# Mixed expert blocks without register loads, answers fetched in 2 KB pieces, and a wider GpSimd add in the first combine

## The reference, cut to what matters

```python
def ffn(x):                      # x normalised, 4096 x 256
    scores = sigmoid(x @ gate.T)                         # 32 experts
    topk_idx = top_k(masked(scores + bias), 6)           # 6 experts per token
    for e in range(32):                                  # gate_up[e]: 256 x 256, down[e]: 256 x 128
        o = (silu(x @ gu[e][:128].T) * (x @ gu[e][128:].T)) @ down[e].T
        routed += combine[:, e] * o                      # zero where e was not chosen
    return routed + (silu(x @ sg.T) * (x @ su.T)) @ sd.T # shared expert
x = x + 0.5 * ffn(layernorm(x))
x = x + local_attention(layernorm(x), segments of 64) + global_attention(segment means)
x = x + 0.5 * ffn(layernorm(x))
```

## Time and profile before

| | |
|---|---|
| median of three runs | 1494.6 us (1494.43 to 1495.4) |
| profiled execution | 1491.28 us, its span 1489.4 us |
| granted TensorE clock | 0.911 of full speed |
| PE busy | 1265.4 us, 85% |
| DVE busy | 1057.8 us, 71% |
| POOL busy | 894.5 us, 60% |
| ACT busy | 720.5 us, 48% |
| DMA, mean | 184 GB/s |
| answers fetched, first combine | 32 DMAs of 512 KB, 32 of 256 KB, about 5 us each from issue to landing |

### The profile page before, as it was taken

How to read it: one execution, slowest core, us unless ns; L and a number is a source line. 1 busy time by engine, 2 the same in 40 slices (tenths; PEclk the granted TensorE clock), 3 DMA queues, 4 the chain that set the end, 5 groups by cost and what they waited for, 6 DMA issues and landing times. The chain is left out here.

```text
span 1489.4 us, 47447 instructions
## 1 busy us (share of the span) xinstructions
PE 1265.4 (85%) x10480; PEld 1077.5 (72%) x10481; DVE 1057.8 (71%) x5308; ACT 720.5 (48%) x2232; POOL 894.5 (60%) x949
## 2 busy tenths in 40 slices
PE   6876662699999999789989989942999999999984
PEld 5765661599999996478766767732999999984864
DVE  6676656488888886477478888864788888874775
ACT  3433320466666665300467666721666666664100
POOL 3777777466666665332027776774666666654786
PEclk8777775799999999999799999955999999999998
DMA  9963333466666665597013333453666666653896
GB/s 312 404 263 128 128 128 128 138 189 187 188 190 189 188 190 167 162 329 249 2 47 133 141 137 129 147 190 132 183 192 190 189 189 193 189 181 112 301 317 221
DMA packets 154761, 274.44 MB, mean 184 GB/s; under 512 B 27942, under 2 KB 107067, under 8 KB 154688
## 3 DMA queue, kind: packets, MB, share of 16 engines
q1 hardware_dynamic: 116288, 160.27, 35.2%
q0 software_dynamic: 38400, 113.31, 20.5%
HBM read 146.59 MB, written 131.07 MB: 186 GB/s over the span
## 5 line engine op out<-in xcount | busy, mean ns | idle before, releaser
L772 PE MATMUL ps<-xbt,ans 128*128 128x128 f32 x3072 | 409.2, 276 | 0.2
L772 PEld LDWEIGHTS ps<-xbt,ans 128*128 128x128 f32 x3072 | 376.3, 193 | 1.3 <-ACT ans L1375 0.8
L733 POOL DMA_INDIRECT answers<-yb,didx x208 | 204.9, 985 | 159.2 <-issue 102.4
L733 POOL DMA_INDIRECT answers<-ans,didx x208 | 204.8, 985 | 128.8 <-issue 87.6
L717 POOL DMA_INDIRECT dispatch_rows<-blk,idx x192 | 190.6, 993 | 137.1 <-issue 121.9
L1375 ACT COPY ans<-wgu 128x512 f32 x416 | 255.2, 614 | 0.2 <-issue 0.2
L1864 DVE SCALAR_TENSOR_TENSOR picked<-iota_e,etab,blk 128x32 f32<-128x32 f32 x832 | 177.0, 250 | 102.7 <-DVE yb L1885 36.4
L693 POOL DMA_INDIRECT dispatch_rows<-blk,idx x192 | 188.0, 979 | 78.3 <-issue 58.1
L772 PE MATMUL ps<-wdn,hb 128*128 x768 | 229.6, 381 | 0.0
L1385 ACT ACTIVATE sg<-ps 128x128 f32<-128x128 f32 x416 | 115.8, 278 | 210.0 <-PE ps L772 206.5
L1367 ACT COPY xbt<-ps 128x256 f32<-128x256 f32 x416 | 153.9, 370 | 76.7 <-PE ps L895 76.6
(11 more groups left out here) (272 smaller groups left out, 2188.5 us busy)
## 6 DMA issues: line engine op xcount, KB each, us to landing
blk<-dispatch_rows SPq DMA_DIRECT2D x384, 160.0 KB
ans<-answers SPq DMA_DIRECT2D x54, 512.0 KB, 5.0
ans<-answers SPq DMA_DIRECT2D x54, 256.0 KB, 5.0
wgu<-in_gate_up SPq DMA_DIRECT2D x32, 256.0 KB
dispatch_rows<-blk,idx POOLq DMA_INDIRECT x384
dispatch_rows<-padt SPq DMA_DIRECT2D x32, 160.0 KB
blk<-dispatch_rows SPq DMA_DIRECT2D x64, 80.0 KB
yb<-answers SPq DMA_DIRECT2D x10, 512.0 KB, 5.3
```

The lines of the kernel that those rows point to most:

```text
L733: pool.indirect_dma_start(out=answers_dram, out_offset=bass.IndirectOffsetOnAxis(ap=didx[:, q:q + 1], axis=0), in_=block_answers(q), in_of ...
L772: return nc.tensor.matmul(out_, lhs, rhs, start=start, stop=stop)
```

## The change

It has three parts.

**Mixed blocks.** SP, PE and ACT hold all the register values of the 16 mixed blocks in registers of their own, read from `itab` while whole blocks are still worked on. SP's last 60 whole blocks are written out, and each carries one piece of that: the load of a register or, every other block, one of the first twelve down-weight loads, which now have twelve buffers. The last four follow between mixed row loads. Two semaphores take the place of four: one for the first twelve, one for the last four.

**2 KB pieces.** All fetches of answers are DMAs of 2 KB a partition (256 KB in all), three a tile, in both combines.

**First combine.** There are four buffers. PE sums answers 0 and 1 by two matmuls with the identity. POOL adds answers 2 and 3 to answers 4 and 5 in one instruction of 512 elements. PE adds the first half of that to its sum with one more matmul (`pooled`, issued behind the next tile's `first_two`), and DVE adds the second half to `xres` as before. SP fetches the third piece of tile i when PE (`four`) and DVE (`own`) are done with tile i-4.

```diff
-        def upper_down(k):
-            return vv[:, k, :] if k < 2 else prob[:].rearrange("p h k -> p (h k)")[:, (k - 2) * D:(k - 1) * D]
+        def upper_down(m):
+            k = m % DOWNS
+            if k >= 10:
+                return (xn2, red[:])[k - 10]
+            return (vv[:].rearrange("p k d -> p (k d)"), prob[:].rearrange("p h k -> p (h k)"),
+                    hsh[:].rearrange("p j s -> p (j s)"), ssg[:].rearrange("p j s -> p (j s)"),
+                    flat[:, E * E + 4 * P + 2 * KC * 2 * I:])[k // 2][:, k % 2 * D:(k % 2 + 1) * D]
...
+        held = [flat[:, 0:6 * D], flat[:, 6 * D:], (yb[:].rearrange("p k d -> p (k d)"), vv[:]),
+                (blk[:].rearrange("p q r -> p (q r)"), prob[:])]
...
             def load_mixed(m):
                 n = WHOLE + m
                 freed(n)
                 for k in range(2):
-                    reg = ahead[(2 * m + k) % 16]
                     sp.dma_start(block_rows(n % LOADS)[k * SEG:(k + 1) * SEG, :],
-                                 rows_dram[bass.ds(row_of(reg), SEG), :]).then_inc(s.ld[n % LOADS], 16)
-                    if m + 8 < MIXED:
-                        fetch(reg, WHOLE + 2 * (m + 8) + k)
+                                 rows_dram[bass.ds(row_of(ahead[2 * m + k]), SEG), :]).then_inc(s.ld[n % LOADS], 16)
...
-            for k, n in enumerate(range(WHOLE - 4 * LOADS, WHOLE)):
-                load(n, n % LOADS, m=0)
-                fetch(ahead[k], WHOLE + k)
-            for m in range(4):
-                load_down(m)
-            for m in range(MIXED + 4):
-                if m < MIXED:
-                    load_mixed(m)
-                if m >= 8:
-                    load_down(m - 4)
+            for n in range(WHOLE - peeled, WHOLE):
+                load(n, n % LOADS, m=0)
+                k = n - (WHOLE - peeled)
+                if k < 2 * DOWNS:
+                    (load_down if k % 2 else fetch_upper)(k // 2)
+                elif k < DOWNS + MIXED:
+                    fetch_upper(k - DOWNS)
+                else:
+                    fetch(ahead[k - (DOWNS + MIXED)], WHOLE + k - (DOWNS + MIXED))
+            for m in range(MIXED):
+                load_mixed(m)
+                if 9 <= m < 9 + MIXED - DOWNS:
+                    load_down(DOWNS + m - 9)
...
             for i in range(NT):
-                j = i % 3
-                positive(sp, s.four, i - 2)
-                sp.dma_start(sums_of[j][0], ans_v[i][:, 0:4 * D]).then_inc(s.ans[0][j], 16)
-                positive(sp, s.own, i - 2)
-                sp.dma_start(sums_of[j][1], ans_v[i][:, 4 * D:]).then_inc(s.ans[1][j], 16)
+                j = i % 4
+                two = lambda k: ans_v[i][:, 2 * k * D:(2 * k + 2) * D]
+                positive(sp, s.two, i - 3)
+                sp.dma_start(two_of(j, 0), two(0)).then_inc(s.ans[0][j], 16)
+                positive(sp, s.pair, i - 3)
+                sp.dma_start(two_of(j, 1), two(1)).then_inc(s.ans[1][j], 16)
+                positive(sp, s.four, i - 3)
+                positive(sp, s.own, i - 3)
+                sp.dma_start(two_of(j, 2), two(2)).then_inc(s.ans[1][j], 16)
...
         def pool_sum(pool, s):
             for i in range(NT):
-                two = sums_of[i % 3][1]
-                pool.wait_ge(s.ans[1][i % 3], 16 * (i // 3 + 1))
-                pool.tensor_tensor(two[:, 0:D], two[:, 0:D], two[:, D:], ALU.add).then_inc(s.pair, 1)
+                pool.wait_ge(s.ans[1][i % 4], 32 * (i // 4 + 1))
+                pool.tensor_tensor(two_of(i % 4, 2), two_of(i % 4, 1), two_of(i % 4, 2), ALU.add).then_inc(s.pair, 1)
...
-                for k in range(4):
-                    m = mm(ps[:, q, 0:D], ident[:], four[:, k * D:(k + 1) * D], start=(k == 0), stop=(k == 3))
-                m.then_inc(s.four, 1)
+                for k in range(2):
+                    m = mm(ps[:, q, 0:D], ident[:], two_of(i % 4, 0)[:, k * D:(k + 1) * D], start=(k == 0), stop=False)
+                m.then_inc(s.two, 1)
+
+            def pooled(i, q):
+                pe.wait_ge(s.pair, i + 1)
+                mm(ps[:, q, 0:D], ident[:], two_of(i % 4, 2)[:, 0:D], start=False).then_inc(s.four, 1)
...
-            act.wait_ge(C0.own, NT - 2)
+            act.wait_ge(C0.own, NT - 1)
+            act.wait_ge(C0.four, NT - 1)
```

More of the change, by code:

```diff
@@ L361, in __init__ @@
                     self.sh_x = s("sh_x")
-        LOADS, ANSWERS = 4, 8
+        LOADS, ANSWERS, DOWNS = 4, 8, 12
         row_loads = [sem(f"ex_ld{q}") for q in range(LOADS)]
-        down_loads = [sem(f"ex_dn{q}") for q in range(4)]
+        first_downs, last_downs = sem("ex_first_downs"), sem("ex_last_downs")
         class ExpertSems:
@@ L412, in __init__ @@
                 s = lambda name: sem(f"{name}_0")
-                self.ans = [[s(f"cs_ans{part}_{j}") for j in range(3)] for part in range(2)]
+                self.ans = [[s(f"cs_ans{part}_{j}") for j in range(4)] for part in range(2)]
+                self.two = s("cs_two")
                 self.four = s("cs_four")
@@ L524, in sp_experts @@
             first = [sp.alloc_register(f"first{k}_{s.n}") for k in range(2)]
-            ahead = [sp.alloc_register(f"first_half{k}_{s.n}") for k in range(16)]
+            ahead = [sp.alloc_register(f"first_half{k}_{s.n}") for k in range(2 * MIXED)]
             def fetch(reg, n):
@@ L885, in pe_experts @@
             expert = [pe.alloc_register(f"expert{j}_{s.n}") for j in range(2)]
-            lower = [pe.alloc_register(f"lower_expert{j}_{s.n}") for j in range(3)]
+            lower = [pe.alloc_register(f"lower_expert{j}_{s.n}") for j in range(MIXED)]
             pe.wait_ge(s.tab, 1)
@@ L956, in step @@
                     pe.reg_load(expert[1 - j], itab[0:1, bass.ds(n - 1, 1)])
-                if m is not None and WHOLE <= n + 1 < NB:
-                    mixed_expert(n + 1)
+                if m is not None and WHOLE <= n + MIXED < NB:
+                    mixed_expert(n + MIXED)
             tx(0, 0)
@@ L967, in pe_experts_run @@
                 step(n, n, m=0)
-            with pe.Fori(1, WHOLE // 8 - 1) as g:
+            with pe.Fori(1, (WHOLE - MIXED) // 8) as g:
                 for q in range(8):
                     step(g * 8 + q, q)
-            for n in range(WHOLE - 8, NB + 2):
+            for n in range(WHOLE - MIXED, NB + 2):
                 step(n, n % 8, m=0)
@@ L1025, in pe_sum @@
             for i in range(NT):
-                body(i, i % 4)
+                first_two(i, i % 4)
+                if i:
+                    pooled(i - 1, (i - 1) % 4)
                 if i >= 10:
@@ L1035, in pe_sum @@
                     pe_qk(pe, 2, 1, 0, 0, FIRST_K)
+            pooled(NT - 1, (NT - 1) % 4)
             mean(NT - 10)
@@ L1369, in act_experts, with stage @@
             expert = [act.alloc_register(f"staged_expert{j}_{s.n}") for j in range(2)]
-            def stage(n, j):
-                e = act.snap(expert[j], min_val=0, max_val=E - 1)
+            upper = [act.alloc_register(f"staged_upper{j}_{s.n}") for j in range(MIXED)]
+            def stage(n, j, m):
+                mixed = m is not None and n >= WHOLE
+                e = act.snap(upper[n - WHOLE] if mixed else expert[j], min_val=0, max_val=E - 1)
                 positive(act, s.gu, n - 1)
@@ L1391, in step @@
                     xt_copy(n + 2, j)
-                if m is not None and WHOLE <= n + 3 < NB:
-                    act.reg_load(expert[1 - j], itab[0:1, bass.ds(2 * (n + 3) - WHOLE + 1, 1)])
-                elif m is None or n + 3 < NB:
+                if m is None or n + 3 < WHOLE:
                     act.reg_load(expert[1 - j], itab[0:1, bass.ds(n + 3, 1)])
+                if m is not None and WHOLE <= n + MIXED + 4 < NB:
+                    act.reg_load(upper[n + MIXED + 4 - WHOLE], itab[0:1, bass.ds(2 * (n + MIXED + 4) - WHOLE + 1, 1)])
             act.wait_ge(s.tab, 1)
@@ L1401, in act_experts @@
             xt_copy(0, 0)
-            stage(0, 0)
+            stage(0, 0, 0)
             xt_copy(1, 1)
-            stage(1, 1)
+            stage(1, 1, 0)
             act.reg_load(expert[0], itab[0:1, 2:3])
@@ L1407, in act_experts @@
                 step(n, n, m=0)
-            with act.Fori(1, WHOLE // 4 - 1) as g:
+            with act.Fori(1, (WHOLE - MIXED) // 4 - 1) as g:
                 for q in range(4):
                     step(g * 4 + q, q)
-            for n in range(WHOLE - 4, NB):
+            for n in range(WHOLE - MIXED - 4, NB):
                 step(n, n % 4, m=0)
@@ L1904, in own @@
                 v.wait_ge(s.pair, i + 1)
-                v.tensor_tensor(xtile(i), sums_of[i % 3][1][:, 0:D], xtile(i), ALU.add).then_inc(s.own, 1)
+                v.tensor_tensor(xtile(i), two_of(i % 4, 2)[:, D:], xtile(i), ALU.add).then_inc(s.own, 1)
             def stats_of(i):
```

55 lines of the change are left out of this document (30 added, 25 removed).

## The result

| | before | with the change |
|---|---|---|
| median of 20 runs | 1492.19 us (1480.58 to 1495.96) | 1497.7 us (1490.0 to 1504.03) |
| ratio | | 1.0038, 95% interval 1.0023 to 1.0052 |
| profiled execution | 1491.28 us | 1492.44 us |

The change makes the kernel 5.5 us slower. The forecast was -0.3 us, so it was wrong in sign, and the case that I called C, +5.8 us, is what the time looks like. It doesn't follow that C's mechanism is what happened, and it isn't quite. The time itself, 1497.7 us, lies inside the forecast's own range of 1489.5 to 1499, but by luck: the kernel before came out 2.4 us lower in 20 runs than in the three that the forecast started from. Note that the change's profiled execution lies 5.3 us under its own median, while that of before lies 0.9 under.

What follows compares the result with a forecast made beforehand. It took late loads to stall PE at mixed blocks, a three-buffer fetch loop to bound the first combine, and POOL the second. -8.2 + 7.5 + 0.4 = -0.3 us gave 1494.3 us, range 1489.5 to 1499.

Steps and rivals of the forecast that it cites:

- C: First combine: every POOL add holds DVE for all of its 1.08 us, 3.025 us a tile; 1500.4 us, chance 0.22.
- Mixed blocks, -8.2: End of both expert stages: moving down-weight and register loads away removes PE's waits and the irregular steps behind them, -8.2 us.
- rival D: Last 60 whole blocks of each layer: SP falls behind with the moved loads, +6 us; about 1500.3 us, chance 0.04.
- First combine, +7.5: First combine: POOL's longer add holds up DVE, which becomes the bound at 2.79 us a tile; +7.5 us in all.
- -2.05 forecast: Start of the first combine: four tiles fetched at once bring tile 5's `own` to 636.3 instead of 638.35, -2.05 us.
- +8.4 and +0.7 forecast: First combine: 26 tiles at 2.79 instead of 2.467 us, +8.4; two normalised tiles made in between by DVE, +0.7.
- +0.4 forecast: End of the first combine: it now stands behind POOL's last add and one more matmul, +0.4 us.
- A: First combine: POOL's adds don't hold DVE up and the DMA sets the pace, -10 us; 1476.8 us, chance 0.12.
- B: First combine: DVE loses no more than today, 0.54 us a tile, -0.5 us; 1486.3 us, chance 0.22.
- PE has room: First combine: eight identity matmuls and first waits, read as two tiles, take 1.83 us, so PE is not the bound.
- Second combine, +0.4: Second combine: three 2 KB DMAs a tile cost only a slightly later last tile, since POOL is full; +0.4 us.
- As POOL is full: Second combine: POOL's adds and the gaps between them fill 35.2 of 35 us, 2.84 us a tile.

Runs made afterwards that it cites:

- the gaining parts: Kernel before plus the mixed part, four buffers, 2 KB pieces and POOL's 256-element add in the first combine; second combine as before: ratio 0.9973, again 0.9901.
- the last two kernels of the table: Kernel before plus the gaining parts, run again with 2 KB fetches in the first combine (0.9901), and the same with one 4 KB fetch there (0.9876).

## Why the prediction was wrong

- **Mixed blocks, -8.2.** Right in mechanism, 1.3 us too small: -9.5. Two whole steps come first, as forecast, but the next two took 1.86 and 1.93 us instead of 2.22. The moved loads slowed nothing: whole blocks stay at 1.55 us, rival D is out. (Why the second expert's down weights need a copy is stated ahead of the prediction; no run here tests it.)
- **First combine, +7.5.** Right, +7.9. The add takes 1.27 us, as forecast; DVE loses 0.9 us a tile (0.85 forecast) and needs 1.9 itself (1.945 forecast). From block 207 to tile 5 it took 27.4 us instead of 29.3 (-1.8; -2.05 forecast), from there to tile 31 +9.75 (+8.4 and +0.7 forecast), and the end took nothing more (3.22 us in both; +0.4 forecast). The Trainium skill's rule of the shared port pair ("SBUF — State Buffer", section "SBUF: two separate sides") agrees with the 1.25 against 0.17 us. Of DVE's operations in these tiles, the BATCH_NORM_STATS2 and the adds with an input in PSUM were never more than 0.02 us longer than their shortest. A and B are out; C too as a mechanism, since DVE loses 0.9 and not 1.08 us a tile.
- **"PE has room"** was misread from the earlier trace rows. It did not move the sum, as three matmuls a tile and the means (1.4 + 0.4 us) left the bound with DVE. But it hid that PE was near its bound before (2.2 of 2.467 us), and the kernel with all six sums on PE was built on it.
- **Second combine, +0.4: this is the step that failed.** "As POOL is full" was read from 35 us of the stage. Over the whole of it POOL already waited 11.0 us for DVE before, and DVE 16.3 for answers. So POOL was not full and nothing hid a later answer; in the change's profile both waits grew, to 16.8 and 18.5 us. The term measured +2.8 in the pair of profiles, and that turns the sum of the terms positive. How much of it is the pieces stays open: with this part alone it was +0.9, over all kernels +1.3 as a mean.
- **The sum.** -9.5 + 7.9 + 2.8 = +1.2 us. The two profiled executions differ by just that, but this is luck. Two stretches that the sum leaves out cancel: the first routing, which the change leaves alone, took 1.9 us less in the change's profile, and the join took 2.0 us more. Against the 5.5 us of the medians the terms leave 4.3 us that I could not place. For the version of the gaining parts the same sum came out near (-16.4, measured -14.8).
- **The join** had no term at all. When the first combine ends, PE may be on its lower clock. In the change's profile the last means took 3.58 us, where they were 2.03; before, then now:

```profile
705.85 2.03 PE L772 MATMUL ps<-share_rstd,xres 128*128 128x2 f32 x16 [1.25 <-DVE minus_mean L1933]
```

```profile
707.04 3.58 PE L794 MATMUL ps<-share_rstd,xres 128*128 128x2 f32 x16
```

How long that lasts varies between like kernels. Of the last two kernels of the table, which differ in one fetch's size, here are the two windows of 10 us that begin about 5 us after the last tile sum. First the one with 324.5 us of join, then that with 335.8:

```profile
698.00:708.00 10.00, 9.85 (x102) 8.52 (x103) 5.16 (x23) 4.57 (x21) 0.00 (x0) 0.85 0.01 2
708.00:718.00 10.00, 9.34 (x162) 6.96 (x161) 4.80 (x13) 7.25 (x37) 0.00 (x0) 1.00 0.01 3
```

```profile
697.30:707.30 10.00, 10.00 (x58) 8.48 (x56) 3.92 (x19) 3.55 (x18) 0.00 (x0) 0.50 0.01 2
707.30:717.30 10.00, 10.00 (x98) 7.88 (x96) 1.61 (x4) 3.67 (x20) 0.00 (x0) 0.60 0.01 2
```

The one regains the higher clock there, the other stays at half of it (0.50) for ten us and more, and the joins are 11 us apart. The other traces show the same, nearly in order. By the granted clock between 10 and 20 us after the last tile sum:

| clock there | join, 1850 us chips | join, 1495 us chip |
|---|---|---|
| 1.00 | 406.9 to 408.7 (5 traces) | 324.5 |
| 0.93 to 0.97 | 410.7, 411.8 | 330.4 (the change) |
| 0.61 | 412.2 | 328.4 (before) |
| 0.50 | 414.7 to 419.0 (7 traces) | 335.8 |

The mixed part alone, run twice, stands in the first row and in the last (407.5 and 416.4). So this spread, up to 12 us, belongs to a run and not to a kernel, and one pair of profiles can't say what the change does to the join. The change lowers the granted clock in the first combine from 0.96 to 0.86, with PE waiting for DVE, and one could think that it meets the long join more often. Its three traces (330.4, 406.9 and 410.7 us) don't bear that out: all seven long joins on the 1850 us chips are those of other kernels. The 4.3 us stay open.

## What to carry to other kernels

Count a tile's matmuls in the trace against the program before calling an engine idle: one matmul here is two entries. Read a stage's bound over its whole length, not in its best stretch. Here a longer POOL add beside a DVE that was nearly busy was paid for by DVE almost in full (0.9 of 1.08 us): price a moved addition by what it holds up, not by its own engine's idle time. Before a sum of terms is called confirmed by a pair of profiles, take the difference of the stretches that the change leaves alone as well.

## What the runs showed of the hardware

- A POOL add of 256, 512 and 8 elements a partition took 0.73, 1.27 and 0.20 us.
- With such adds beside them, DVE's operations were longer than their shortest by 0.91 us a tile (512 elements), 0.32 (256) and 0.02 (8); an operation of four elements took up to 1.26 us instead of 0.16.
- Fetching in 2 KB pieces ran at 374 GB/s in the first combine with the 8-element add, above the 364 of the earlier trace rows.
- SP's queue issued a DMA of the answers every 0.48 us, so six a tile took 2.9 us (1 KB pieces).
- Between 10 and 20 us after the first combine the granted clock of TensorE was 0.50 of full speed in seven of the 15 traces on the 1850 us chips and 1.00 in five, and the stretch behind it was 6 to 12 us longer in the seven. One and the same kernel was found in both groups, 9 us apart.
- One program took 1495 us on one chip and 1850 on others: +194 us in whole expert blocks, +79 in each of the two stretches with routing, nothing in the combines. ACT stood still up to 3.2 us between blocks there. Why is open.
